# A feed-forward stage with experts: one sequence of dense and sparse items, lists ahead of the sparse ones, the zeros written inside the stage

## The reference

```python
capacity = max(1, int(Sz * CAP_FACTOR / E) + 1)      # 257 tokens of 1024, 8 experts
scores = softmax(einsum('bsd,ed->bse', x, router_w))
gate_vals, sel_idx = top_k(swapaxes(scores, 1, 2), capacity)
tokens = x[b_idx, sel_idx]
h = gelu(einsum('becd,edh->bech', tokens, w1) + b1, approximate=False)   # 128 -> 512
y = einsum('bech,ehd->becd', h, w2) + b2                                 # 512 -> 128
out = zeros_like(x).at[b_idx, sel_idx].add(y * gate_vals[..., None])
```

## Time and profile before

| | |
|---|---|
| median of three runs | 1023.42 us |
| profiled execution | 1025.62 us, span of its instructions 1023.9 us |
| TensorE busy | 822.4 us (80%) |
| VectorE busy | 638.9 us (62%) |
| ScalarE busy | 536.5 us (52%) |
| GpSimd busy | 363.9 us (36%) |
| 48 scatters, line 1373 | 79.3 us busy on GpSimd, 3.3% of the span on the chain that ended last |
| 48 gathers, line 1365 | 60.2 us busy on GpSimd |

### The profile page before, as it was taken

The page is one execution under the profiler, slowest core; times in us unless marked ns, Lnnn a source line. Parts: engine busy times, 40 slices in busy tenths (PEclk is TensorE's granted clock), DMA queues, the critical chain, the costliest instruction groups (busy, mean ns, idle before and its releaser), DMA issues. The chain is left out here.

```text
span 1023.9 us, 15516 instructions
## 1 busy us (share of the span) xinstructions
PE 822.4 (80%) x5714; PEld 522.9 (51%) x5714; DVE 638.9 (62%) x1168; ACT 536.5 (52%) x980; POOL 363.9 (36%) x595
## 2 busy tenths in 40 slices
PE   1888999999998889589217898999999888969930
PEld 1554566555654667488214333444444346748830
DVE  3786677777674468684125877777777555867521
ACT  0614666666667478256105256666666667825620
POOL 1071336654333100357835112123322130034784
PEclk9998999999999989789759799999999999977975
DMA  6572432232011401225323371111000022122434
GB/s 179 123 248 52 134 84 77 80 94 77 18 64 42 124 4 43 64 84 140 34 54 101 86 184 33 33 33 33 1 2 2 2 72 56 42 63 82 133 40 100
DMA packets 59003, 74.65 MB, mean 73 GB/s; under 512 B 11552, under 2 KB 46064, under 8 KB 58544
## 3 DMA queue, kind: packets, MB, share of 16 engines
q1 hardware_dynamic: 45136, 62.47, 20.9%
q0 software_dynamic: 8576, 6.53, 4.7%
q10 hardware_dynamic: 5216, 4.66, 1.6%
HBM read 42.24 MB, written 30.29 MB: 71 GB/s over the span
## 5 line engine op out<-in xcount | busy, mean ns | idle before, releaser
L1110 ACT ACTIVATE b_pt<-b_banks 128x512 f32<-128x512 f32 (+1 forms) x320 | 154.6, 560 | 102.0 <-PE b_banks L1024 101.8
L1133 DVE TENSOR_REDUCE a_mlate<-a_banks 128x2 f32<-128x1024 f32 (+3 forms) x120 | 124.8, 1080 | 51.1 <-PE a_banks L962 32.6
L1133 DVE TENSOR_REDUCE b_mlate<-b_banks 128x2 f32<-128x1024 f32 (+3 forms) x120 | 126.1, 1081 | 35.0 <-PE b_banks L962 18.3
L1024 PE MATMUL a_banks<-a_q,a_k 121*128 121x512 f32 (+3 forms) x384 | 117.0, 382 | 5.2 <-DMA a_q<-a_mt 4.3
L1110 ACT ACTIVATE a_q_hl<-a_banks 128x512 f32<-128x512 f32 (+1 forms) x160 | 81.8, 557 | 67.9 <-PE a_banks L1024 66.4
L1110 ACT ACTIVATE a_k_hl<-a_banks 128x512 f32<-128x512 f32 (+1 forms) x160 | 82.1, 557 | 53.5 <-PE a_banks L1024 52.0
L962 PE MATMUL a_banks<-a_k,a_q 120*128 120x512 f32 (+3 forms) x384 | 99.1, 360 | 11.4 <-DVE a_mlate L1133 7.6
L1024 PE MATMUL b_banks<-b_q,b_k 64*128 64x512 f32 (+3 forms) x384 | 98.4, 414 | 12.1 <-ACT b_pt L1110 8.7
L1024 PEld LDWEIGHTS b_banks<-b_q,b_k 64*128 64x128 f32 x384 | 47.3, 186 | 88.0 <-ACT b_pt L1110 54.5
L1637 ACT ACTIVATE f_h<-f_banks,b_t 128x512 f32<-128x512 f32 (+1 forms) x112 | 74.2, 684 | 33.9 <-PE f_banks L1546 26.0
L1024 PEld LDWEIGHTS a_banks<-a_q,a_k 121*128 121x128 f32 x384 | 65.1, 190 | 50.5 <-issue 20.3
(11 more groups left out here) (253 smaller groups left out, 1378.3 us busy)
## 6 DMA issues: line engine op xcount, KB each, us to landing
scratch_w<-a_tab SPq DMA_DIRECT2D x16, 512.0 KB, 3.1
f_w1r<-scratch_w SPq DMA_DIRECT2D x16, 512.0 KB
f_w2r<-scratch_w SPq DMA_DIRECT2D x16, 512.0 KB
a_rot<-in_w SPq DMA_DIRECT2D x16, 256.0 KB, 3.7
a_q<-scratch_q SPq DMA_DIRECT2D x8, 384.0 KB
a_k<-scratch_k SPq DMA_DIRECT2D x8, 384.0 KB
scratch_q<-b_q_hl SPq DMA_DIRECT2D x24, 128.0 KB, 2.9
b_q<-scratch_q SPq DMA_DIRECT2D x32, 96.0 KB
```

What stands on the lines that cost most here:

```text
L1024: last = pe.matmul(st[u % NST][:, col:col + w], head_rows(k2, n, h, slice(key * P, (key + 1) * P), 1), head_rows(q2, n, h, slice(c * CH + ...
L1110: act.activation(pt[at % NPT][:, h, 0:cols], st[u % NST][:, 0:cols], ACT.Exp, scale=scale).then_inc(exp_done, 1)
L1133: last = dve.tensor_reduce(dst, src, AX.X, ALU.max, negate=True)
```

## The change

The stage becomes one sequence of 17 items: ten dense chunks, five sparse experts, two dense chunks (three experts are dense now, five sparse). Units run through all of it. Every use of the spare banks gets a unit (`SPARE_AT`), and VectorE's list is sorted by the same units: the first list stands at unit 59, the last at 85, the sparse items begin at unit 76, the turns back and with them the scatters stand at units 94 to 125. The third dense expert has weight buffers of its own. The zeros are written by SyncE inside the stage, behind the scores, and GpSimd's first gather waits for them too. The gated rows are written over the gathered ones (`xg`) in place of `yg`. The reload is shared by SyncE and ScalarE.

```diff
-KEEP = 2
+KEEP = 3
...
+AHEAD = 10
+
+ITEMS = [("dense", q) for q in range(AHEAD)] + [("some", s) for s in range(ROUTED)]
+ITEMS += [("dense", q) for q in range(AHEAD, DENSE)]
+ITEM = {item: n for n, item in enumerate(ITEMS)}
...
+def blocks_of(n):
+
+    hidden = [("hidden", n, j) for j in range(HB)] if n < len(ITEMS) else []
+    output = [("output", n - 1, j) for j in range(HB)] if n else []
+    if n < AHEAD or n == len(ITEMS):
+        return hidden + output
+    return hidden[0:2] + output[0:2] + [hidden[2], output[2], hidden[3], output[3]]
...
+def unit_of(n):
+
+    return 8 * n - 4 if n else 0
...
+SPARE_AT = [(57, ("odd_index",)), (59, ("index", 0)), (66, ("index", 1)), (72, ("index", 2)), (73, ("rows", 0)),
+            (79, ("index", 3)), (81, ("rows", 1)), (83, ("turn", 0)), (85, ("index", 4)), (87, ("turn", 4)), (89, ("rows", 2)),
+            (91, ("turn", 1)), (94, ("back", 0)), (95, ("turn", 5)), (97, ("rows", 3)), (99, ("turn", 2)), (102, ("back", 1)),
+            (103, ("turn", 6)), (105, ("rows", 4)), (107, ("twins",)), (107, ("turn", 3)), (110, ("back", 2)),
+            (111, ("turn", 7)), (115, ("turn", 8)), (118, ("back", 3)), (123, ("turn", 9)), (125, ("back", 4)),
+            (129, ("odd_turn",)), (130, ("odd_sum",)), (133, ("turn", 10)), (135, ("turn", 11))]
+HOT_AT = {1: 61, 2: 68, 3: 75, 4: 81}
...
+def low_units(n):
+
+    u = unit_of(n)
+    if n == 6:
+        return RANK, RANK
+    if n < AHEAD - 1:
+        return beside_step(u + 5), beside_step(u + 8) if n else 8
+    if n == AHEAD - 1:
+        return u + 5, u + 8
+    return (u + 4, u + 8) if n < len(ITEMS) - 1 else (u + 4, u + 7)
...
+WEIGHT_USERS = [[0] + list(range(KEEP, NE, 2)), [1] + list(range(KEEP + 1, NE, 2)), [2]]
+WEIGHTS_OF = {e: i for i, users in enumerate(WEIGHT_USERS) for e in users}
...
-                sp.wait_ge(made, 4)
-                for sums in m.sums:
-                    sp.dma_start(sums[0:B * T, :].rearrange("(t p) d -> p t d", p=P),
-                                 zeros[:, :].rearrange("p (o d) -> p o d", o=1).to_broadcast([P, NT, D])).then_inc(loaded, 16)
-                sp.wait_ge(loaded, 16 * (NCH + 8))
+                sp.wait_ge(loaded, 16 * (NCH + 6))
...
-    yg = sb("yg", [P, ROUTED, PER_EXPERT, D])
...
+    rows_stored = 16 * (NCH + B + 1)
...
-        for what, i in LOADS:
-            if what == "first":
-                matrix(i, 0, w1r)
-            else:
-                matrix(i, 1, w2r)
-        sp.wait_ge(scattered[0], scattered_by(ROUTED) + 16)
-        for c in range(NCH):
-            if c == NCH // B:
-                sp.wait_ge(scattered[1], scattered_by(ROUTED))
-            sp.dma_start(m.v[:, c * TPC:(c + 1) * TPC, :], by_chunk(sums[0:B * T, :], c)).then_inc(m.x_in[c], 16)
+        sp.dma_start(sums[0:B * T, :].rearrange("(t p) d -> p t d", p=P),
+                     m.zeros[:, :].rearrange("p (o d) -> p o d", o=1).to_broadcast([P, NT, D])).then_inc(rows_out, 16)
+        for e in range(2, NE):
+            for w in range(2):
+                matrix(e, w)
+        reload(sp, 0)
...
+    def reload(eng, b):
+        eng.wait_ge(scattered[0], scattered_by(ROUTED) + 16)
+        eng.wait_ge(scattered[1], scattered_by(ROUTED))
+        for c in range(b * NCH // B, (b + 1) * NCH // B):
+            eng.dma_start(m.v[:, c * TPC:(c + 1) * TPC, :], by_chunk(sums[0:B * T, :], c)).then_inc(m.x_in[c], 16)
...
-                pool.indirect_dma_start(out=sums, out_offset=row(s, c), in_=yg[:, s, c, :], in_offset=None,
+                pool.indirect_dma_start(out=sums, out_offset=row(s, c), in_=xg[s][:, c, 0:D], in_offset=None,
...
         u = 0
-        for q in range(DENSE):
-            for j in range(HB):
-                hidden(q, j)
+        for n in range(len(ITEMS) + 1):
+            for what, i, j in blocks_of(n):
+                if what == "hidden":
+                    hidden(i, j)
+                else:
+                    output(i, j)
                 routing(u)
+                beside(u)
                 u += 1
-            if q:
-                for j in range(HB):
-                    output(q - 1, j)
-                    routing(u)
-                    u += 1
...
+        for n in range(len(ITEMS)):
+            if n >= 2:
+                keep(n - 2)
             for j in range(HB):
-                bend(q, j, q // NCH, CH, h_ps[:, j, :])
+                bend(n, j)
                 if j % 2:
-                    high(q, j, CH)
-            if q:
-                keep(q - 1)
-        keep(DENSE - 1)
-        rows_high(0)
-        for s in range(ROUTED + 2):
-            if s >= 2:
-                keep_some(s - 2)
-            if s >= ROUTED:
-                continue
-            q, e = DENSE + s, KEEP + s
-            for j in range(HB):
-                bend(q, j, e, PAIR, h_ps[:, 2 * (j % 2):2 * (j % 2) + 2, 0:SLOTS])
-                if j % 2:
-                    high(q, j, PAIR)
-                if j == 2 and s + 1 < ROUTED:
-                    rows_high(s + 1)
+                    high(n, j)
+                if j == 2 and ("rows", n - AHEAD + 1, 0) in SPARE and n >= AHEAD:
+                    rows_high(n - AHEAD + 1)
+            if n == AHEAD - 1:
+                rows_high(0)
+        keep(len(ITEMS) - 2)
+        keep(len(ITEMS) - 1)
+        reload(act, 1)
...
-            columns = m.steps[:, len(SHIFTS) * PLANES + P:].rearrange("p (o c j) -> p o c j", o=1, j=2)
-            link(dve.tensor_tensor(part_of[:, :, :].rearrange("p (t c) j -> p t c j", c=BE),
-                                   third[:, :, :].rearrange("p t (c o) -> p t c o", o=1).to_broadcast([P, TT, BE, 2]),
-                                   columns.to_broadcast([P, TT, BE, 2]), ALU.is_equal))
-            dve.tensor_scalar(parts[:, :, 0, :], part_of[:, :, :], m.token[:, 0:1], None, ALU.mult)
-            dve.tensor_tensor(parts[:, :, 1, :], part_of[:, :, :],
-                              m.tile_row[:, :].rearrange("p (c o) -> p c o", o=1).to_broadcast([P, TT * BE, 2]), ALU.mult
-                              ).then_inc(hot_ready, 1)
+            of_all = third[:, :, :].rearrange("p t c -> p (t c)")
+            for j in range(2):
+                dve.tensor_scalar(parts[:, :, 0, j], of_all, float(j), m.token[:, 0:1], ALU.is_equal, ALU.mult)
+                last = dve.scalar_tensor_tensor(out=parts[:, :, 1, j], in0=of_all, scalar=float(j), in1=m.tile_row[:, :],
+                                                op0=ALU.is_equal, op1=ALU.mult)
+            last.then_inc(hot_ready, 1)
...
-            dve.tensor_tensor(yg[:, s, :, :], spare(("back", s)).rearrange("p (c d) -> p c d", d=D),
+            dve.tensor_tensor(xg[s][:, :, 0:D], spare(("back", s)).rearrange("p (c d) -> p c d", d=D),
...
+            dve.wait_ge(spare_done, spare_uses("turn", DENSE - NCH + c))
```

More of the change, by code:

```diff
@@ new lines, with spare_order, spare_count @@
+HOT_AT = {1: 61, 2: 68, 3: 75, 4: 81}
+def spare_order():
+    order = []
+    for _, key in SPARE_AT:
+        if key[0] == "rows":
+            order += [("gap", key[1])] * (len(order) % 2 == 0) + [(*key, 0), (*key, 1)]
+        else:
+            order.append(key)
+    return order
+SPARE_ORDER = spare_order()
+SPARE = {key: i for i, key in enumerate(SPARE_ORDER)}
+BESIDE_UNIT = {u: [key for at, key in SPARE_AT if at == u] for u, _ in SPARE_AT}
+def spare_count(i):
+    return sum(key[0] != "gap" for key in SPARE_ORDER[:i])
@@ L1521, in hidden, with output @@
             last.then_inc(h_mm, 1)
[L1523 to L1524 removed]
+        def output(n, j):
+            e, w = expert_of(n), w2r[WEIGHTS_OF[expert_of(n)]]
             if j == 0:
[L1526 to L1536 removed]
@@ L1550, in output_some @@
[L1550 to L1561 removed]
+                pe.wait_ge(m.w_in[1][WEIGHTS_OF[e]], weights_in(e))
```

360 lines of the change are left out of this document (160 added, 200 removed).

## The result

The changed kernel takes 977.73 us, the median of three runs (976.41 to 978.48), against 1023.42 before: a ratio of 0.9543 with the interval 0.9514 to 0.9572. It is faster by 46 us, where 60 were forecast. The profiled execution has 978.48 us with a span of 976.6, so the span lost 47.3 us. These lie as follows.

What follows compares the result with a forecast made beforehand. Some 35 us of each stage were bound by late scatters, not arithmetic, with further losses at entrance and start. Gains of 6 (start) + 27 + 27 (stages) = 60 us against 1023.4 gave 963 us, range 949 to 989.

Steps and rivals of the forecast that it cites:

- The start: Kernel start: constants no longer wait for two 1 MB zero writes; gains 6 us, bounds 3 and 8.4.
- The entrance: Routing's last group to first sparse matmuls: sparse items start at 429.2 instead of 431.3, with two more dense chunks done.
- First sparse matmuls to the first scatter: Sparse part's beginning: items start at 429.2, first turn back stands at 449.4, first scatter goes out at 451.
- The scatters: Beside the sparse experts: four take 8.7 us, between 7.5 and 10.0; the five experts' scatters end at 494.5.
- Landing and odd scatter: Stage end: last scatter lands 2.6 us after its end; odd scatter to the reload's issue takes 2.7.
- The reload: Stage end: issue to last addition takes 6.65 us less about 0.9 for two queues instead of one.
- The sum of the first stage: Stage ends at 505.4 instead of 531.9, gaining some 27 us; low bound 20, high 33.
- GpSimd is held by VectorE: Rival at the scatters: each subtraction blocks one for 1.23 us, an expert takes 10.0; 977 us, chance 0.18.
- In-order waits: Rival: each of the last eight items waits 2 us instead of 0.5, stage gains 15; 987 us, chance 0.16.
- The overlap fails: Rival: scatters bunch up behind TensorE, stages gain nothing and only the start stays; 1017 us, chance 0.06.
- Slower: Rival: added dense chunks run at the lower clock, up to 60 us more per stage; 1083 us, chance 0.04.
- signs named for being right: First VectorE instruction near 10; first scatter about 42 us behind slot routing, scatters spread; TensorE end idle about 12 us.

Runs made afterwards that it cites:

- e1: Changed kernel with the zeros written among the constants again instead of inside the stages; 981.29 us.
- e5: Changed kernel with the first expert's list used for all five and the four later comparisons replaced by a 16-element memset; 962.90 us.
- e4: Changed kernel with the first expert's list used for all five and the four later comparisons replaced by one-source reductions over as many elements; 959.48 us.
- e6: Changed kernel with the reload of the sums issued by SyncE alone instead of two queues; 974.84 us.
- e8: Changed kernel with comparisons 2 to 4 and their lists moved behind the first expert's gathers, and the reload on SyncE alone; 971.66 us.
- e10: Changed kernel with comparisons 1 to 4 each made by 16 one-source instructions, and the reload on SyncE alone; 982.95 us.
- e2: Changed kernel with GpSimd holding the first scatter until the last expert's rows are scaled; 1029.79 us.

## Why the prediction was right and where it was wrong

The sign holds, and so does the mechanism: scatters beside the sparse experts, an earlier start. 977.7 lies inside the range, but the forecast of 963 is 15 us too low. Step by step:

- **The start.** 6 forecast, 6.3 measured at the first VectorE instruction (10.13; the text had "near 10"). The 6 was a choice between bounds of 3 and 8.4, and no run separates the two reasons behind them, so its closeness is in part luck. Writing the zeros inside the stage was priced at nothing, and e1 shows it so.
- **The entrance is the step that failed.** The prediction ended it with "A miss costs 1 to 3 us". It cost 6.9 in each stage. The prediction looked for the miss in VectorE's length. e5 shows that this length costs nothing, and e4 that all of the miss is GpSimd being held: 5.6 us of waiting and 2.0 at the lower clock that followed the wait. The term that was mis-sized is the stretch from GpSimd's first gather to the rows. It was taken from the old kernel as 9.05 us (418.32 to 427.37 in the earlier trace rows) and set against 11.3 us of cover on TensorE; after the change it measures 14.28, and 8.66 in e4. The old stretch holds only for what ran on VectorE beside it then: there one gather was held, for 1 us. The new order set two comparisons and three subtractions beside exactly the gathers that TensorE waits for. So the entrance, which was to become 2.1 us shorter, became 4.8 longer.
- **First sparse matmuls to the first scatter.** 21.8 forecast, 21.5 measured.
- **The scatters.** 43.5 forecast for the twenty, 41.45 measured; 8.3 us for four in place of 8.7, between the bounds of 7.5 and 10.0, and nearer to the low one. Both chains arrive together, as forecast (492.97 and 491.03).
- **Landing and odd scatter.** 2.56 and 2.67 us, as priced.
- **The reload.** 5.75 forecast, 8.02 measured, 2.3 too little. The 0.9 taken off for two queues had the wrong sign (e6). One queue took 7.46 and 6.59 in e6, 7.10 and 6.33 in e8, 6.47 and 6.49 in e10, so the old row of 6.65 was near.
- **The sum of the first stage.** 6.9 − 0.3 − 2.05 + 2.3 = 6.8 us above the forecast, which is what the two profiles show (103.7 against 96.9). In the second it is 6.5 (103.4).

The rivals: *GpSimd is held by VectorE* gave 977, and the time is 977.7. That agreement is half a coincidence. The hold is real and it is what took the missing gain, but the rival set it at the scatters, where four take 8.3 us and not its 10.0. It struck the gathers at the entrance, of which no case spoke. I had the mechanism, with its row, and applied it to one of the two places where GpSimd issues beside VectorE. *In-order waits*: behind the entrance TensorE is idle for 3 us of 62.9 (21.21 of 21.4 and 38.65 of 41.5 us busy), and the longest wait between experts at the scatters is 1.33 us, so no. *The overlap fails*: e2 is that case, built, and it costs 53 us. *Slower*: the sparse part has a clock of 0.98 and 0.99, so no; behind the routing the lower level shows only behind the wait at the entrance and at the empty end (0.50 both times). One of the signs named for being right did not come: the first scatter stands 49 us behind the routing's last group (402.51 to 451.52) and not 42, by the 7 us of the entrance.

## What to carry to other kernels

When work is moved, price not only the moved instruction but every instruction of another engine that it now stands beside: a row's duration, or a stretch between two rows, holds for its old neighbours. If a mechanism of contention has a row in the trace, walk through every place of the new order where the two engines meet, first of all where a third engine waits for the result. A replacement with the same length but other access, as e4's reduction, tells contention from length in one run. And look in the old trace for the same pair of engines at the same place: the gather at 419.91 showed the hold before anything was built.

## What the runs showed of the hardware

- An indirect gather of 128 rows is 0.94 us of GpSimd when VectorE leaves it alone. Behind comparisons and subtractions that follow each other without a gap one became 3.04, and the odd rows' gather, 1.22 beside a reduction, became 4.56. The indirect scatter with addition went from 1.55 to 2.64 at most.
- Who began first counts: a gather under way when the comparison began was not held by it (418.32 in the kernel before, 1.28 us), one that began inside it was held until about its end (419.91, 1.96 us).
- A subtraction on VectorE with both sources in SBUF holds a gather that begins inside it (1.40 us at 434.67 in the kernel after); one with a source in PSUM does not (0.94 at 437.62).
- A wait of 5.58 us on TensorE was followed by 5 us of matmuls at a granted clock of 0.50: six 512-column matmuls 2.93 us, against 1.65 where the wait was gone and the clock 1.00. So the wait cost 7.6 us and not 5.6.
- A reload of four pieces took longer when its issue was shared by two queues: 7.2 to 8.0 us from the issue to the last addition, against 6.3 to 7.5 on one queue, over all profiles here.
